# Attention: the norms' constant added on GpSimd, one power for two norms, and the maxima folded in two groups of four

## The reference

```python
def _layernorm(x, eps=1e-05):               # of a row
    return (x - mean(x)) / sqrt(var(x) + eps)

xn  = _layernorm(_layernorm(x)) * ln1_g + ln1_b        # "first norm"
q, k, v = split(xn @ in_proj_w.T + in_proj_b)          # 16 heads of 8
scores  = q @ k.T / sqrt(8) + mask                     # causal, with relative positions
o   = softmax(scores) @ v                              # needs each row's maximum
y   = _layernorm(x) + o @ out_w.T + out_b
y   = y + relu(_layernorm(y) * g + b @ w1.T + b1) @ w2.T + b2    # "second norm"
x   = x + y
x   = x + ffn(_layernorm(x))                           # "row norm", then router, top 2 of 8 experts
```

## Time and profile before

| | us |
|---|---|
| time, median of 3 runs (1423.67 to 1427.74) | 1425.31 |
| the profiled execution's own time | 1423.46 |
| its span, first to last instruction | 1421.7 |
| PE busy over the span | 1150.5 (81%) |
| DVE busy | 1146.0 (81%) |
| ACT busy | 979.1 (69%) |
| POOL busy | 935.3 (66%) |

### The profile page before, as it was taken

How to read it: one execution, slowest core, us unless ns; L and a number is a source line. 1 busy time by engine, 2 the same in 40 slices (tenths; PEclk the granted TensorE clock), 3 DMA queues, 4 the chain that set the end, 5 groups by cost and what they waited for, 6 DMA issues and landing times. The chain is left out here.

```text
span 1421.7 us, 38123 instructions
## 1 busy us (share of the span) xinstructions
PE 1150.5 (81%) x11753; PEld 972.4 (68%) x11753; DVE 1146.0 (81%) x3840; ACT 979.1 (69%) x2078; POOL 935.3 (66%) x1004
## 2 busy tenths in 40 slices
PE   4789999999999999998559999757677636999950
PEld 2567777777777777776449999745455525999940
DVE  5488999999999999997558888569889855887758
ACT  3588888888888888886146666358778734666630
POOL 5235577877877777866747777426888884777740
PEclk8699999999999999999669999779989967999975
DMA  7311111111111111110423333112222212333338
GB/s 205 101 49 46 41 57 56 62 63 64 53 59 54 62 64 63 57 47 22 145 75 106 107 107 105 50 60 74 78 76 78 63 59 73 107 107 102 102 113 286
DMA packets 99444, 117.20 MB, mean 82 GB/s; under 512 B 17785, under 2 KB 79793, under 8 KB 99249
## 3 DMA queue, kind: packets, MB, share of 16 engines
q1 hardware_dynamic: 70560, 73.57, 17.4%
q0 software_dynamic: 16896, 35.16, 7.2%
q10 hardware_dynamic: 11792, 6.05, 1.5%
HBM read 47.56 MB, written 41.51 MB: 63 GB/s over the span
## 5 line engine op out<-in xcount | busy, mean ns | idle before, releaser
L1166 DVE TENSOR_TENSOR ebuf<-score_banks,region 128x768 f32<-128x768 f32 x256 | 243.7, 952 | 19.1 <-PE score_banks L869 14.4
L1415 ACT ACTIVATE region<-ebuf 128x768 f32<-128x768 f32 x256 | 216.5, 862 | 22.0 <-DVE ebuf L1166 21.9
L1393 ACT CAST copied<-max_banks 128x768 bf16<-128x768 f32 x251 | 202.6, 807 | 16.0 <-PE max_banks L857 13.6
L1834 POOL DMA_INDIRECT choice_rows<-first_yo,first_xg x136 | 130.6, 960 | 67.7 <-PE first_by L1872 42.2
L1834 POOL DMA_INDIRECT choice_rows<-second_yo,second_xg x136 | 130.3, 958 | 63.3 <-PE second_by L1872 39.9
L1688 POOL DMA_INDIRECT expert_rows<-d_rows,a_d_index x112 | 132.0, 1178 | 31.0 <-issue 17.1
L912 PE MATMUL bankO<-region,vaug 128*32 128x256 f32 (+1 forms) x2048 | 110.9, 334 | 1.9 <-ACT region L1415 1.9
L1594 POOL TENSOR_TENSOR rs<-arg,neghalf 128x4 f32<-128x4 f32 x32 | 37.1, 1161 | 110.1 <-DVE arg L1098 110.1
L860 PE MATMUL max_banks<-region_r 32*128 32x256 f32 x502 | 97.9, 386 | 11.3 <-DMA region_r<-region_r 5.5
L1910 ACT ACTIVATE first_silu<-first_bgu,first_biases 128x256 f32<-128x256 f32 (+1 forms) x144 | 66.6, 463 | 57.5 <-issue 29.9
L833 PE MATMUL max_banks<-identb,region 128*128 128x128 bf16 x502 | 99.9, 224 | 4.6 <-ACT copied L1393 4.5
(11 more groups left out here) (374 smaller groups left out, 4395.3 us busy)
## 6 DMA issues: line engine op xcount, KB each, us to landing
region_r<-region_r SPq DMA_DIRECT2D x192, 128.0 KB
first_xg<-expert_rows SPq DMA_DIRECT2D x64, 132.0 KB
second_xg<-expert_rows SPq DMA_DIRECT2D x64, 132.0 KB
z_rows<-choice_rows SPq DMA_DIRECT2D x32, 256.0 KB
c_rows<-choice_rows SPq DMA_DIRECT2D x16, 512.0 KB
out<-xres ACTq DMA_DIRECT2D x16, 256.0 KB
choice_rows<-first_yo,first_xg POOLq DMA_INDIRECT x136
choice_rows<-second_yo,second_xg POOLq DMA_INDIRECT x136
```

Source lines behind the costliest of these rows:

```text
L1166: nc.vector.tensor_tensor(ebuf[:, half_of_ebuf(c, j), :, :], score_banks[:, :, 0:BK], bias32[:, plain(j), :], ALU.add).then_inc(scores_fre ...
L1393: nc.scalar.copy(copied[:, 2 * j:2 * j + 2, :], banks_of_max(c, j)[:, :, 0:BK]).then_inc(maxed_free, 1)
L1415: nc.scalar.activation(p32[:, j % 4, :, :], ebuf[:, half_of_ebuf(c, j), :, :], ACT.Exp).then_inc(exped, 1)
L1834: pool.indirect_dma_start(choice_dram, bass.IndirectOffsetOnAxis(ap=xg[:, i % G, t, E:E + 1].bitcast(I32), axis=0), yo[:, i % 4, t, :], No ...
```

## The change

Three things are changed.

1. DVE no longer adds EPS. POOL does it, with a TENSOR_SCALAR just ahead of each power, and waits for its own result in between: one for the second norm, two for the first norm and the row norm together.
2. The power of the row norm (`row_root`) is gone; `roots` takes it together with that of the first norm, on six columns instead of four and two. In POOL's body the row norm's power thereby moves from before `norm_apply` to after it.
3. `FOLDS` has two groups of four pairs in place of groups of three, three and two. The second `fold_keys`/`fold_half` of a body, which stood between `place_a`, `norm_moments` and `place_d`, is gone, and the last group, at the top of the body, has four pairs.

The lists of PE, ACT and SP are unchanged.

```diff
-    neghalf = sb("neghalf", [P, 4])
+    neghalf = sb("neghalf", [P, 6])
...
-    FOLDS = ((0, 3), (3, 6), (6, 8))
+    FOLDS = ((0, 4), (4, 8))
...
+    def row_slot(c):
+        return (c + 7) % RING
...
             def norm_moments(c, n):
...
-                    last = ch.mark(nc.vector.bn_aggr(mv[:, n, t, :], stats[:, t, :]))
-                ch.wait(last)
-
-                if some(c):
-                    dve.wait_ge(rs1_ready, c)
-                nc.vector.tensor_scalar(arg[:, 0, :], mv[:, n, :, 1], 1.0, EPS, ALU.mult, ALU.add)
-                nc.vector.tensor_scalar(arg[:, 1, :], mv[:, n, :, 1], 1.0 + EPS, EPS * EPS, ALU.mult, ALU.add).then_inc(arg1_ready, 1)
+                    nc.vector.bn_aggr(mv[:, n, t, :], stats[:, t, :]).then_inc(mv_ready, 1)
...
             def second_moments(c):
...
-                nc.vector.tensor_scalar(arg2[:], mv2[:, :, 1], 1.0, EPS, ALU.mult, ALU.add).then_inc(arg2_ready, 1)
+                    nc.vector.bn_aggr(mv2[:, t, :], stats2[:, t, :]).then_inc(mv2_ready, 1)
...
             def row_moments(c):
...
-                nc.vector.tensor_scalar(arg3[:], mv3[:, :, 1], 1.0, EPS, ALU.mult, ALU.add).then_inc(arg3_ready, 1)
+                    nc.vector.bn_aggr(mv[:, row_slot(c), 2 + t, :], stats3[:, t, :]).then_inc(mv3_ready, 1)
...
             def body(b):                       # DVE
-                fold_keys(b, 2)
-                fold_half(b, 2)
+                fold_keys(b, 1)
+                fold_half(b, 1)
...
                 place_a(b - 5)
-                fold_keys(b + 1, 1)
                 norm_moments(b + 4, (b + 4) % RING)
                 place_b(b - 5)
                 place_c(b - 5)
-                fold_half(b + 1, 1)
                 place_d(b - 5)
...
+            def roots(c, r):                   # POOL
+                n, lo, hi = c % RING, 0 if exists(c) else 2, 4 if exists(r) else 2
+                if exists(c):
+                    pool.wait_ge(mv_ready, 2 * c + 2)
+                    if some(c - RING + 1):
+                        pool.wait_ge(xn_ready, c - RING + 1)
+                        pool.wait_ge(xl_ready, c - RING + 1)
+                    ch.mark(nc.gpsimd.tensor_scalar(arg[:, 4:6], mv[:, n, 0:2, 1], 1.0 + EPS, EPS * EPS, ALU.mult, ALU.add))
+                if exists(r):
+                    pool.wait_ge(mv3_ready, 2 * r + 2)
+                    if some(r - RING + 1):
+                        pool.wait_ge(d_normed, r - RING + 1)
+                ch.step(nc.gpsimd.tensor_scalar(arg[:, lo:hi], mv[:, n, lo:hi, 1], 1.0, EPS, ALU.mult, ALU.add))
+                ...
+                nc.gpsimd.tensor_tensor(rs[:, n, lo:hi], arg[:, lo:hi], neghalf[:, lo:hi], ALU.pow).then_inc(rs_ready, 1)
...
             def second_root(c):
...
+                ch.step(nc.gpsimd.tensor_scalar(arg2[:], mv2[:, :, 1], 1.0, EPS, ALU.mult, ALU.add))
                 nc.gpsimd.tensor_tensor(rs2[:], arg2[:], neghalf[:, 0:2], ALU.pow).then_inc(rs2_ready, 1)
...
             def body(b):                       # POOL
...
                 residuals(b - 2)
-                row_root(b - 3)
                 norm_apply(b + 3, (b + 3) % RING)
-                roots(b + 4, (b + 4) % RING)
+                if exists(b + 4) or exists(b - 3):
+                    roots(b + 4, b - 3)
```

More of the change, by code:

```diff
@@ L1082, in norm_stats @@
                     dve.wait_ge(x_in[X_PARTS.index(2 * c)], 16)
+                if some(c):
+                    dve.wait_ge(mv_ready, 2 * c)
                 for t in range(2):
@@ L1195, in second_norm @@
                 dve.wait_ge(W_free, useW("att", c) + 1)
+                if some(c):
+                    dve.wait_ge(mv2_ready, 2 * c)
                 for t in range(2):
@@ L1203, in second_moments @@
                 for t in range(2):
-                    last = ch.mark(nc.vector.bn_aggr(mv2[:, t, :], stats2[:, t, :]))
-                ch.wait(last)
-                if some(c):
-                    dve.wait_ge(rs2_ready, c)
-                nc.vector.tensor_scalar(arg2[:], mv2[:, :, 1], 1.0, EPS, ALU.mult, ALU.add).then_inc(arg2_ready, 1)
+                    nc.vector.bn_aggr(mv2[:, t, :], stats2[:, t, :]).then_inc(mv2_ready, 1)
             def finish(c):
@@ L1238, in row_moments @@
                 for t in range(2):
-                    last = ch.mark(nc.vector.bn_aggr(mv3[:, t, :], stats3[:, t, :]))
-                ch.wait(last)
-                nc.vector.tensor_scalar(arg3[:], mv3[:, :, 1], 1.0, EPS, ALU.mult, ALU.add).then_inc(arg3_ready, 1)
+                    nc.vector.bn_aggr(mv[:, row_slot(c), 2 + t, :], stats3[:, t, :]).then_inc(mv3_ready, 1)
             def sort(c):
@@ L1585, in _ @@
         def _(pool):
-            def roots(c, n):
-                if not exists(c):
-                    return
-                pool.wait_ge(arg1_ready, c + 1)
-                if some(c - RING + 1):
-                    pool.wait_ge(xn_ready, c - RING + 1)
-                    pool.wait_ge(xl_ready, c - RING + 1)
-                nc.gpsimd.tensor_tensor(rs[:, n].rearrange("p a t -> p (a t)"), arg[:].rearrange("p a t -> p (a t)"),
-                                        neghalf[:], ALU.pow).then_inc(rs1_ready, 1)
+            ch = Chain(pool, gchain)
+            def roots(c, r):
[11 more added lines that the diff above has]
+                ch.step(nc.gpsimd.tensor_scalar(arg[:, lo:hi], mv[:, n, lo:hi, 1], 1.0, EPS, ALU.mult, ALU.add))
+                hi = 6 if exists(c) else hi
+                if hi == 6 and not exists(r):
+                    ch.mark(nc.gpsimd.tensor_tensor(rs[:, n, 4:6], arg[:, 4:6], neghalf[:, 4:6], ALU.pow))
+                    hi = 2
+                nc.gpsimd.tensor_tensor(rs[:, n, lo:hi], arg[:, lo:hi], neghalf[:, lo:hi], ALU.pow).then_inc(rs_ready, 1)
             def norm_apply(c, n):
@@ L1604, in norm_apply @@
                 for t in range(2):
-                    last = nc.gpsimd.tensor_scalar(xn[:, t, :], tile(c, t), mv[:, n, t, 0:1], rs[:, n, 1, t:t + 1],
+                    last = nc.gpsimd.tensor_scalar(xn[:, t, :], tile(c, t), mv[:, n, t, 0:1], rs[:, n, 4 + t:5 + t],
                                                    ALU.subtract, ALU.mult)
@@ L1615, in normed_input @@
                 for t in range(2):
-                    last = nc.gpsimd.tensor_scalar(xlb[:, n, t, :], tile(c, t), mv[:, n, t, 0:1], rs[:, n, 0, t:t + 1],
+                    last = nc.gpsimd.tensor_scalar(xlb[:, n, t, :], tile(c, t), mv[:, n, t, 0:1], rs[:, n, t:t + 1],
                                                    ALU.subtract, ALU.mult)
@@ L1646, in residuals @@
                                         tiles(c).rearrange("p t e -> p (t e)"), ALU.add).then_inc(ysum_ready, 1)
-            def row_root(c):
-                if not exists(c):
-                    return
-                pool.wait_ge(arg3_ready, c + 1)
-                if some(c):
-                    pool.wait_ge(d_normed, c)
-                nc.gpsimd.tensor_tensor(rs3[:], arg3[:], neghalf[:, 0:2], ALU.pow).then_inc(rs3_ready, 1)
             def row_apply(c):
@@ L1666, in row_apply @@
                         pool.wait_ge(scattered[k][g % 2], 64 * (g // 2 + 1))
+                n = row_slot(c)
                 for t in range(2):
-                    last = nc.gpsimd.tensor_scalar(d.rows[:, c % DEPTH, t, 0:s.E], tile(c, t), mv3[:, t, 0:1], rs3[:, t:t + 1],
+                    last = nc.gpsimd.tensor_scalar(d.rows[:, c % DEPTH, t, 0:s.E], tile(c, t), mv[:, n, 2 + t, 0:1], rs[:, n, 2 + t:3 + t],
                                                    ALU.subtract, ALU.mult)
```

23 lines of the change are left out of this document (12 added, 11 removed).

## The result

The changed kernel takes 1490.13 us (median of 4 runs, 1484.42 to 1491.66). The kernel before takes 1426.53 (median of 4 runs). The ratio is 1.0448, 95% interval 1.0417 to 1.048: 4.5% slower. The profiled execution took 1489.12 us, 65.7 more than that of before.

A forecast was written before the change was run, and what follows sets the result against it. PE's own work plus a few turns PE to ACT to PE was taken to set the pace. 1423.46 + 56.4 - 0.5 - 1.4 + 0.5 = 1478.5, plus 1.85 to the runs' median: 1480 us; range 1461 to 1502.

The forecast's parts named there:

- the signs named: Profile after: DVE idle about 2.3 us before L1123, PE about 1.8 before L864, body about 21 us, PE near 86%, POOL waiting longer.
- The wait for copy 3: First fold_keys (L1123) of a body now needs ACT's copy 3 (L1393), which ends 2.36 us after the fold starts now.
- The chain behind it: Copy 3, fold, L192, q, second fold, mask of pair 0, then PE's fill 1: PE stands still 1.82 us per body.
- The give-back of 0.11 us in 13 bodies: PE's 0.37 us wait for DVE before fill 5 goes, worth 0.11 us in some 13 bodies: -1.4 us.
- The two folds behind the mask of pair 4: They grow, but three instructions of 0.61 take 1.83 us where 2.05 passed, so nothing new is late at pair 5.
- POOL: covered: POOL's added work, between -0.3 and +1.9 us a body, is covered by its waits of 2.3 and 1.6 us before the powers.
- The addition ahead of the second norm: POOL's addition of up to 0.72 us would eat the 0.5 us before PE's L964, but fill 1's 1.82 us delay covers it.
- PE's clock is left out: No clock term for PE: at 17.20 of 20 us busy it was granted 1.00 as well.
- DVE sets the pace: Rival: DVE, busy 19.03 of 20 us, bounds the kernel and the change makes it faster, 1393 us; chance 4%.
- Nothing measurable: Rival: the wait for copy 3 is there but covered, leaving only 0.11 us in 13 bodies, 1424 us; chance 3%.
- Absorption: Rival: PE's 0.66 us wait for ACT before L925 shrinks as all becomes later, 36 us lost, 1460; chance 10%.
- Collision with POOL: Rival: wider first-group folds run beside POOL's L1634 and lose 0.4 us each, 1505 us, or 1492 with one; chance 13%.

The follow-up runs named there:

- the rest alone: The changed kernel with the three fold groups of the kernel before put back, leaving EPS on POOL and the common power: 1425.32 us, ratio 1.0027.
- the later folds: The changed kernel with the first group's fold_keys moved behind the mask of pair 1 and fold_half behind the first norm's moments: 1428.06 us, ratio 1.002.
- both fillings: The changed kernel with fill 1's bias matmuls made five times instead of once (1477.3 us), and with them made three times (1488.03 us).
- the kernel before with the filling: The kernel before with fill 1's bias matmuls made five times instead of once, where PE does not wait: 1467.6 us, ratio 1.0294.
- three and five pairs: The changed kernel with two fold groups of three and five pairs instead of four and four: 1431.3 us, ratio 1.0053.
- the folds alone: The kernel before with only the two groups of four pairs; EPS stays on DVE, the row norm keeps its own power: 1487.01 us, ratio 1.0448.
- q first: The changed kernel with the choice of experts and the lower half of q moved ahead of the first group's folds: 1479.02 us, ratio 1.0367.
- fully filled: The changed kernel with fill 1's six bias matmuls made five times instead of once during PE's wait: 1477.3 us, ratio 1.0373.
- half filled: The changed kernel with two more sets of bias matmuls in fill 1 in place of four: 1488.03 us, ratio 1.0409.

## Why the prediction was right, point by point

The forecast was 1480, the range 1461 to 1502; it is 1490. Sign, mechanism and place are as predicted. The size is 10 us short. Of the signs named, DVE's and PE's waits and the body of 21 us are there; PE's busy share in the steady part is 88% (484.94 of 551.0), where 86 was expected.

- **The wait for copy 3: right.** 2.36 us predicted from the earlier trace rows, 2.28 measured; copy 3 ends 2.59 us after PE's L802 or L806 starts, before and after alike, so it didn't move.
- **The chain behind it: right, a little too long.** The fold cost 0.61, L192 0.13 in every second body, q 0.40, the second fold 0.60, the mask 0.95, as sized. DVE went on after 0.03. Only PE's going on was too dear: 405.22 is 0.06 after the mask ends at 405.16, where 0.10 stood in the sum. L864 came 1.67 us later in the one kind of body and 1.80 in the other, against 1.82.
- **The give-back of 0.11 us in 13 bodies: right that it is next to nothing.** In the runs with the rest alone and with the later folds PE's wait of 0.37 us before fill 5 is gone, and the bodies still take 19.31 us, so it bought nothing. PE's wait for outT shrank a little: 10.1 us in 440 where it was 14.4 before, with 17 rows in place of 22. Per body (21.04 and 19.32 us long) that is 0.48 and 0.63. So 0.15 was absorbed, not the 0.66 of that rival.
- **The two folds behind the mask of pair 4 were mis-sized, without effect.** I took 0.61 for each of the three instructions there, 1.83 in all. Each of the two folds is followed by an instruction that reads its result, and L1144 takes 0.82 beside POOL's row norm (L1668) where it took 0.69 without it (202.89): 0.72 + 0.72 + 0.75 = 2.19 us pass from L1123 at 413.63 to the mask at 415.82. PE doesn't wait for that mask.
- **POOL: covered, as predicted.** The groups by form, 120 to 660 us:

```profile
L1641 POOL TENSOR_SCALAR xm<-y,mv,rs 128x128 f32<-128x128 f32 x52 | 52.3, 1010 | 2.7
L1601 POOL TENSOR_TENSOR rs<-arg,neghalf 128x6 f32<-128x6 f32 x25 | 33.9, 1354 | 2.1
...
L1596 POOL TENSOR_SCALAR arg<-mv 128x4 f32<-128x4 f32 x25 | 4.8, 193 | 2.1
L1591 POOL TENSOR_SCALAR arg<-mv 128x2 f32<-128x2 f32 x25 | 4.8, 191 | 91.4 <-DVE mv L1098 91.4
```

  An addition costs 0.19 us, where only bounds (nothing to 0.72) were to be had. The power of six columns costs 1.35 in place of the estimated 1.60. POOL waits 91.4 / 25 = 3.7 us a body ahead of them, longer than the 2.3 of before, as predicted. The addition ahead of the second norm did not show, not even with the rest alone, where no wait for copy 3 covers it (a steady part of 502.2 us against 501.8).
- **The term that was left out without a good reason is PE's clock ("PE's clock is left out").** It rested on one early window that was granted 1.00 although PE was busy for only 17.20 of 20 us. A share over 20 us doesn't tell one long wait from many short ones. Against the profiled execution 55.0 us were predicted (1478.5 - 1423.46). The waits make the 26 steady bodies 26 x 1.72 = 44.7 longer; by the same 1.72 the three first bodies that have such a wait come to about 5.2, and the two of the drain (the last one waits 1.04) to 2.8: 52.7, so 2.3 less than predicted. On top come 4.5 us from the five bodies at the lower clock, 3.8 more in the first bodies, 1.8 more in the drain and 2.3 from the later start: 12.4. 52.7 + 12.4 = 65.1. Only the 4.5 is shown to be the clock behind the wait: both fillings took the slow bodies away, and the full one gave back 4.3.
- **The rest of the 12.4 stays open.** For the 3.8 and the 1.8 the clock is only argued. That of the first bodies (0.77 against 0.83) is as low in the trace of the later folds (0.77), which lack those three waits and take 82.6 us there, and filling changed nothing (0.78, 89.5 us); the drain varies as much without the wait. The later start is there before the first body: the set-up matmuls L628, which the change doesn't touch, take 1.44 us from 11.54 on, where they took 0.83 from 11.35 on before. Of twelve traces only those of the kernel before and of the kernel before with the filling start at 32.7 and 32.8; those of the ten kernels with one half of the change or both start between 34.9 and 35.7. So it goes with the change, and why stays open.
- **The rivals.** *DVE sets the pace*: fallen, by three runs in which DVE has 24 to 28 us less to do in the steady part and the bodies stay as long. *Nothing measurable*: fallen. *Absorption*: 0.15 of 0.66 us. *Collision with POOL*: it takes place, but in the changed kernel the other side pays for the first group, so it costs no time there. The two folds of the first group are 0.69 and 0.68 long, as L1144 had been. POOL's second norm runs beside them, with 2.31 us for its two instructions in place of 1.57:

```profile
402.65 2.31 POOL L1641 TENSOR_SCALAR xm<-y,mv,rs 128x128 f32<-128x128 f32 x2
```

It ends at 404.96, and PE reads it with L968 at 406.57, later than before because of the wait for the mask. In the run with the rest alone and in the one with later folds these instructions take 0.83 and 0.80 us each, so it is the folds beside them that make the 1.01 above.

Two sections of the Trainium skill stood beside these rivals. With 19.03 of 20 us busy DVE looked saturated, and grouping brought nothing even where it cost nothing (1.002, 0.9995 to 1.0045). The Trainium skill, Perfetto Trace Analysis, section Optimizing Scalar/DVE Operations, says that grouping can improve throughput if the engine is saturated; no run here shows such a gain. Its other sentence there, that breaking up instructions may let work finish sooner where an engine that isn't saturated makes others wait, agrees in part: it is not the number of groups that counts (three and five pairs: 1.0053), but that the first group needs one copy less, and that is worth some 4% here.

L1641 begins at 402.65, behind the fold of 402.47, and it is L1641 that gets longer. The Trainium skill, SBUF — State Buffer, section Who interferes with whom, says that of a VectorE and a GpSimd instruction that contend, the later one blocks; this pair agrees, and I had applied the rule to the wrong side. The second fold doesn't agree: it begins at 403.61, while the first of the two L1641 is still running (402.65 to 403.89), and keeps its 0.68.

## What to carry to other kernels

A group of operations can start only when the last of its inputs is there: before making it larger, look up which input comes last, when, and what stands behind the group in its engine's list. A share of 95% busy doesn't make an engine the bound; ask whom the others wait for, and if nobody waits for it, work taken off it buys nothing. And a new wait on PE may cost more than its length, since the clock can fall behind it (4.5 of 65 us here); a wait that can't be removed can be filled, if the filling is shorter than the wait.

## What the runs showed that I had not expected

- After a wait of 1.6 to 1.74 us once in 21 us, PE's granted clock fell to 0.50 for some 3 us in 5 of 26 bodies (6 in the folds alone, 2 with q first). Matmuls that compute nothing new, put into the wait, took this away in the profiled executions; fully filled, the kernel was 9.7 to 12.8 us faster, of which the steady part shows 4.3, and half filled no gain in time was measured. Ten of the eleven slow bodies of the changed kernel and the folds alone had the longer of the two waits, but 14 others with it did not become slow, and why stays open.
- A fold of 0.69 us costs 0.61 from start to start when unrelated work stands behind it, and 0.72 when the next instruction reads its result. Moving work out from between two such instructions isn't free, even when the engine is idle otherwise.
- Of a DVE fold and a POOL instruction side by side either can be the one that pays. In the changed kernel it is POOL's second norm (2.31 us for 1.57). With q first it is the second fold (0.82 beside that norm, 0.69 without). With the later folds it is the fold: the first one took 1.11 us at 335.67 where others take 0.68, and POOL had begun a scatter (L1688, 1.09 long) at 335.15, before it, and began a residual (L1652) at 336.28. Which of POOL's operations do this, and when, wasn't tried.

The row of that fold in the timeline of DVE, with the later folds:

```profile
335.67 1.11 DVE L1123 TENSOR_TENSOR copied<-copied 128x1024 bf16<-128x1024 bf16 x1
```
